# Reading the high part of the experts' inner values from the product bank, with a second gelu

## The chip, the cores and the metric

The kernel runs on one core of a Trainium2 chip. The metric is the device time of one execution in microseconds, lower is better. One execution is also recorded by the hardware profiler; all times of engines below come from that record, counted from the start of its span.

## The reference

Two sequences of 1024 rows of 256 numbers go through a first attention layer, a layer norm, a second attention with 16 heads of 128, and a mixture of four experts. The change touches only the experts:

```python
hmid = gelu(einsum('td,edi->tei', x, we1) + be1, approximate=False)   # E = 4, inner 256
eout = einsum('tei,eid->ted', hmid, we2) + be2
out  = einsum('te,ted->td', comb, eout)       # comb: weights of the two best experts, 0 elsewhere
return h + out
```

## The kernel before

The kernel is written engine by engine: each engine has a list of steps in a fixed order, and semaphores (`Event`) tie them together. Every product is made of values split in two: a high part in fp32r and a low part, the fp32 value less the high part. `product` issues three matmuls for one product (high by high, high by low, low by high).

After the attention comes the experts' stage. For each batch `b` (2) and each unit `u` (8: four experts for each of the two chunks of 512 rows) there are

- `expert_in(b, u)` on TensorE (PE): two halves, each of 6 matmuls into one bank of `ps_m`, which holds 128 inner values of the 512 rows. The halves are numbered n = 2u and 2u + 1.
- `middle(b, u)` on ScalarE (ACT), four instructions in this order: `gelu_mid(2u)`, `gelu_mid(2u+1)` (L1088: gelu of the bank plus bias, written in fp32 to the SBUF tile `gelu`, which lies in `work`), then `high_mid(2u)`, `high_mid(2u+1)` (L1100: the high part, from `gelu` to `mid_part(0, ...)`, which lies in `wqk_hi` for even u and in `qk_hi` for odd u).
- `low_mid(b, n)` on GpSimd (POOL, L2107): `gelu` less the high part.
- `expert_out(b, u)` on PE: two halves of 12 matmuls into `ps_s`. It needs the low parts of its unit.
- `mix_bias` (L1656) and `mix` (L1666) on VectorE (DVE): add the bias and the weighted result to `acc`.

`ps_m` has two banks, and all of PE's products that go there take them in turn: expert halves, the gate's logits (`gate_logits`, L620), the transposes of a layer norm (`ln_transpose`, L477), the last head's output (`outputs`). `take_bank` numbers the uses. The use of number k waits until use k - 2 has been read, by the event that the table `freed` names for its kind; for `"mid"` that is the end of `gelu_mid` of that half.

Two more waits matter. `gelu_mid(n)` waits for `low_mid(n-2)`, since `gelu` holds two halves. `high_mid` of a unit waits for `expert_out` of the unit but one before it (`out_mm`), whose high parts lie in the same place.

The order on PE around the stage, written out by hand in `ends()`: in(0,0), a transpose, in(0,1), `outputs(LAST, 1)`, out(0,0), two output projections, `ln_transpose(5, 0)`, out(0,1), in(0,2), `gate_logits(1, 0)`, in(0,3), in(0,4), out(0,2), `ln_transpose(5, 1)`, out(0,3), `gate_logits(1, 1)`, in(0,5), out(0,4), in(0,6), out(0,5), in(0,7), out(0,6), in(1,0), in(1,1), out(0,7), in(1,2), out(1,0), out(1,1), in(1,3), out(1,2), in(1,4), in(1,5), out(1,3), out(1,4), in(1,6), out(1,5), in(1,7), out(1,6), out(1,7).

Of the kernel before, what the change touches and what calls it, by code (L numbers as in the profile page):

```python
# [11 lines left out]
ACT = mybir.ActivationFunctionType  # L12
# [8 lines left out]
EXPERTS, INNER = 4, 256  # L21
# [80 lines left out]
def build(nc, A):  # L102

    with ExitStack() as ctx:
# [6 lines left out]
        def event(name, order, step=1):  # L111
            return Event(sem(name), list(order), step)
# [18 lines left out]
        be1 = vec[:, 12:20].rearrange("p (e i) -> p e i", i=2)  # L131
# [26 lines left out]
        gelu = work[:, 0:2, :]  # L158
# [72 lines left out]
        fold_lo = event("fold_lo", folds)  # L231
# [64 lines left out]
        o_lo = event("o_lo", outs2)  # L296
        rinv_done = event("rinv_done", [(u, c) for u in range(UNITS) for c in range(NC)])
        wo_mm = event("wo_mm", outs4)
        acc_done = event("acc_done", first4 + outs4)
# [5 lines left out]
        gate_got = event("gate_got", chunks)  # L305
# [5 lines left out]
        gelu_done = event("gelu_done", mids)  # L311
        mid_hi_done = event("mid_hi_done", mids)
# [60 lines left out]
        def mid_part(n, u, i):  # L373
            if u % 2 == 0:
                whole = (wqk_hi, wqk_lo)[n][:, :, :, :, :].rearrange("p h j k n -> p (h j k n)")
                return whole[:, i * CH:(i + 1) * CH]
            return (qk_hi, qk_lo)[n][:, 1, 0, i * CH:(i + 1) * CH]
# [3 lines left out]
        def m_bank(*use):  # L381
            return ps_m[:, shared[use] % 2, :]
# [13 lines left out]

        @block.tensor
        def _(pe):
            freed = {"fold": fold_lo, "gate": gate_got, "pv": o_lo, "pvs": acc_done, "wo": acc_done, "mid": gelu_done}

            def take_bank(*use):

# [522 lines left out]
        def _(act):  # L925
# [165 lines left out]
            def high_mid(b, n):  # L1091
                u = n // 2
                act.wait_ge(gelu_done.sem, gelu_done.at(b, n))
                if 8 * b + u >= 2:
                    act.wait_ge(out_mm.sem, 16 * b + 2 * (u - 1))
                elif u == 1:
                    act.wait_ge(s_mm.sem, s_mm.at(LAST, NT - 1))
                else:
                    act.wait_ge(qk_mm.sem, qk_mm.at(LAST, 3))
                act.activation(mid_part(0, u, n % 2), gelu[:, n % 2, :],  # L1100
                               ACT.Copy).then_inc(mid_hi_done.sem, mid_hi_done.up(b, n))

            def middle(b, u):
                gelu_mid(b, 2 * u)
                gelu_mid(b, 2 * u + 1)
                high_mid(b, 2 * u)
                high_mid(b, 2 * u + 1)
# [1366 lines left out]
```

## Time and profile before

| | |
|---|---|
| time, median of 3 runs | 1152.41 us (1150.47 to 1155.04) |
| time of the profiled execution | 1155.01 us |
| its span | 1152.9 us |
| PE busy over the span | 1121.9 us (97%), 7154 matmuls |
| DVE, ACT, POOL busy | 866.1 us (75%), 736.6 us (64%), 637.8 us (55%) |
| chain that ended last | PE 91%, DVE 5% |
| experts' stage | from about 1034 us to the end |

The profiled execution took 2.1 us more than its span, and 2.6 us more than the median. Busy time of PE is that of pipelined matmuls, each counted until its modelled end, so it says where PE stands still rather than how well it is used.

### The profile page before, as it was taken

The page shows a single profiled execution, that of the slowest core. Times are in us where ns is not written, and L with a number is a line of the kernel's source. Part 1 is how long each engine was busy: PE and PEld are TensorE (multiplying, and loading weights), DVE is VectorE, ACT ScalarE, POOL GpSimd, SP SyncE. Part 2 cuts the span into 40 slices and gives each one's busy share as a digit, 9 for nine tenths or more (in the row PEclk, how much of TensorE's full clock was granted, in tenths as well). Part 3 has the DMA queues.
Part 4 walks back from the last instruction along what each step waited for, and adds up shares of the span by engine and source line. Part 5 has one row for each costly group of instructions (what it writes and reads, how often), then busy time and mean ns, then how long its engine had stood idle before and what let it go on. Part 6 is the DMA issues. An engine that isn't in the chain of part 4 may idle for free.

```text
span 1152.9 us, 20493 instructions
## 1 busy us (share of the span) xinstructions
PE 1121.9 (97%) x7154; PEld 1021.8 (89%) x7154; DVE 866.1 (75%) x2016; ACT 736.6 (64%) x1565; POOL 637.8 (55%) x511
## 2 busy tenths in 40 slices
PE   8999999999999999999999999999999999889996
PEld 7998889999999999899999999999999998777995
DVE  6766877777777777777777777777777767867698
ACT  3746766666666666666666666666666665574753
POOL 2225756555655555656555555555555556845663
PEclk9999999999999999999999999999999999899998
DMA  5002222121212121212121212121212111221001
GB/s 170 1 1 78 63 73 55 41 60 38 51 38 60 38 51 38 60 38 51 38 60 37 51 37 61 38 51 38 60 37 51 42 38 46 65 92 37 1 20 55
DMA packets 46301, 56.55 MB, mean 49 GB/s; under 512 B 5940, under 2 KB 29176, under 8 KB 46200
## 3 DMA queue, kind: packets, MB, share of 16 engines
q1 hardware_dynamic: 45368, 54.19, 18.9%
q8 instruction: 58, 0.95, 0.3%
q10 hardware_dynamic: 832, 1.05, 0.3%
q14 instruction: 43, 0.35, 0.1%
HBM read 17.47 MB, written 4.19 MB: 19 GB/s over the span
## 4 chain that ended last, share of the span: by engine, by line
PE 91%; DVE 5%; issue 1%; POOL 1%; ACT 1%; DMA 0%; SPq 0%; POOLq 0%; DVEq 0%; ACTq 0%
PE ps_m L424 56%; PE ps_s L424 22%; PE ps_t L562 11%; PE ps_m L477 1%; PE ps_t L430 1%; DVE acc L1595 1%; DVE rows L1487 0%; DVE pT_lo L1562 0%; DVE stats L1434 0%; PE ps_m L620 0%; DVE acc L1666 0%; DVE ps_s L1555 0%; DVE work L1516 0%; DMA wst<-in_L_ffn_we 0%; DVE acc L1477 0%
## 5 line engine op out<-in xcount | busy, mean ns | idle before, releaser
L2069 POOL TENSOR_TENSOR work<-work,rope 128x512 f32<-128x512 f32 x128 | 166.8, 1303 | 229.2 <-DMA work<-work 229.2
L1562 DVE TENSOR_TENSOR pT_lo<-ps_t,pT_hi 128x512 fp32r<-128x512 f32 (+3 forms) x408 | 210.5, 550 | 40.9 <-ACT pT_hi L1065 38.4
L1065 ACT ACTIVATE pT_hi<-ps_t 128x512 fp32r<-128x512 f32 (+3 forms) x408 | 183.0, 489 | 74.9 <-PE ps_t L562 74.5
L1555 DVE CUSTOM_DVE_ANT_0 ps_s<-ps_s,causal 128x128 f32<-128x128 f32 (+7 forms) x272 | 203.2, 765 | 5.9 <-PE ps_s L424 3.3
L2080 POOL TENSOR_TENSOR qk_lo<-work,qk_hi 128x512 fp32r<-128x512 f32 x128 | 163.0, 1293 | 24.9 <-ACT qk_hi L1022 24.9
L2073 POOL TENSOR_TENSOR work<-work 128x512 f32<-128x512 f32 x128 | 167.4, 1308 | 10.1
L1595 DVE SCALAR_TENSOR_TENSOR acc<-ps_m,rinv,acc 128x256 f32<-128x256 f32 x272 | 118.5, 477 | 61.2 <-PE ps_m L424 61.1
L1016 ACT ACTIVATE work<-ps_m,bqk 128x512 f32<-128x512 f32 x128 | 88.7, 693 | 114.5 <-PE ps_m L424 114.3
L424 PE MATMUL ps_s<-qk_hi 128*128 128x384 f32 (+5 forms) x384 | 140.8, 367 | 2.0 <-POOL qk_lo L2080 1.2
L1058 ACT ACTIVATE prob_b<-ps_s,nmax 128x640 f32<-128x640 f32 (+3 forms) x136 | 130.3, 958 | 19.5 <-DVE nmax L1555 16.1
L424 PE MATMUL ps_m<-pT_hi,v_hi 128*128 128x512 f32 (+2 forms) x384 | 135.2, 352 | 3.4 <-DVE pT_lo L1562 2.5
L424 PE MATMUL ps_m<-pT_lo,v_hi 128*128 128x512 f32 (+2 forms) x384 | 134.1, 349 | 0.0
L424 PE MATMUL ps_m<-pT_hi,v_lo 128*128 128x512 f32 (+2 forms) x384 | 133.9, 349 | 0.0
L424 PE MATMUL ps_s<-qk_lo,qk_hi 128*128 128x384 f32 (+5 forms) x384 | 131.8, 343 | 0.0
L424 PE MATMUL ps_s<-qk_hi,qk_lo 128*128 128x384 f32 (+5 forms) x384 | 131.1, 341 | 0.0
L1516 DVE SCALAR_TENSOR_TENSOR work<-ps_m,bqk,rope 128x512 f32<-128x512 f32 x128 | 95.4, 745 | 47.0 <-ACT work L1016 46.8
L562 PE MATMUL ps_t<-ident,prob_b 128*128 128x128 f32 x884 | 120.3, 275 | 1.6 <-DVE pT_lo L1562 1.5
L562 PEld LDWEIGHTS ps_t<-ident,prob_b 128*128 128x128 f32 x884 | 101.9, 141 | 11.4 <-issue 2.9
L1022 ACT ACTIVATE qk_hi<-work 128x512 fp32r<-128x512 f32 x128 | 79.2, 641 | 40.6 <-POOL work L2073 40.4
L424 PE MATMUL ps_m<-hT_hi,wqk_hi 128*128 128x512 f32 x256 | 103.6, 405 | 0.0
L424 PE MATMUL ps_m<-hT_hi,wqk_lo 128*128 128x512 f32 x256 | 100.8, 394 | 0.0
L424 PE MATMUL ps_m<-hT_lo,wqk_hi 128*128 128x512 f32 x256 | 100.6, 393 | 0.0
(197 smaller groups left out, 2855.2 us busy)
## 6 DMA issues: line engine op xcount, KB each, us to landing
work<-work SPq DMA_DIRECT2D x256, 128.0 KB, 2.3
acc<-in_L_attn_x SPq DMA_DIRECT2D x8, 256.0 KB, 4.4
wst<-in_L_ffn_wq SPq DMA_DIRECT2D x16, 128.0 KB, 2.5
wst<-in_L_ffn_wk SPq DMA_DIRECT2D x16, 128.0 KB, 2.4
wo_st<-in_L_ffn_wo SPq DMA_DIRECT2D x16, 128.0 KB, 2.1
wst<-in_L_ffn_wv SPq DMA_DIRECT2D x8, 256.0 KB, 3.0
x_rows<-acc SPq DMA_DIRECT2D x4, 512.0 KB, 3.5
wst<-in_L_ffn_we SPq DMA_DIRECT2D x8, 256.0 KB, 2.9
```

The source lines that it names most:

```text
L424: ins = pe.matmul(out, lhs[x], rhs[y], start=first and k == 0, stop=last and k == 2)
L562: last = pe.transpose(t_bank(u, i, j)[:, k * P:(k + 1) * P], probs(i)[:, part], ident[:, :])
L1016: act.activation(qb[:, x % 2, :], m_bank("q", u, x), ACT.Identity, bias=bqk[:, j, head_:head_ + 1]).then_inc(qb_done.sem, qb_done.up(u, x))
L1058: act.activation(probs(i), all_scores[:, score_range(i)], ACT.Exp, bias=nmax[:, u % 2, i:i + 1], scale=-1.0, accum_out=rsum[:, u % 2, i:i ...
L1065: act.activation(pT_hi[:, slots, cols], t_bank(u, i, j)[:, 0:size * P].rearrange("p (j q) -> p j q", q=P), ACT.Copy).then_inc(t_hi.sem, t_ ...
L1516: dve.scalar_tensor_tensor(qc[:, ring3(u, x), :], m_bank("q", u, x), bqk[:, j, head_:head_ + 1], cos_t[:, c * CH:(c + 1) * CH], ALU.add, A ...
L1555: dve.tensor_tensor_reduce(s, s, causal[:, T - (i + 1) * P:T], -1.0, ABOVE_ALL, ALU.add, ALU.min, accum_out=nmax[:, u % 2, i:i + 1]).then_ ...
L1562: dve.tensor_tensor(pT_lo[:, slots, cols], t_bank(u, i, j)[:, 0:size * P].rearrange("p (j q) -> p j q", q=P), pT_hi[:, slots, cols].bitcas ...
L1595: last = dve.scalar_tensor_tensor(acc[:, b, tile, :], src[:, t * D:(t + 1) * D], rinv[:, u % 2, tile:tile + 1], acc[:, b, tile, :], ALU.mu ...
L2069: pool.tensor_tensor(qs[:, x % 2, :], qs[:, x % 2, :], sin_t[:, c * CH:(c + 1) * CH], ALU.mult).then_inc(sin_done.sem, sin_done.up(u, x))
L2073: pool.tensor_tensor(qc[:, ring3(u, x), :], qc[:, ring3(u, x), :], qs[:, x % 2, :], ALU.add).then_inc(rope_done.sem, rope_done.up(u, x))
L2080: pool.tensor_tensor(qk_lo[:, u % 2, j, cols], qc[:, ring3(u, x), :], qk_hi[:, u % 2, j, cols].bitcast(F32), ALU.subtract).then_inc(qk_lo_ ...
```

## The change

The high part is no longer converted from the fp32 result in SBUF. It is made by a second gelu of the same bank with the same bias, whose output is fp32r. The first gelu stays, because POOL needs its fp32 result for the low part. The bank is therefore read twice, and it counts as free only when the second reading is done.

```diff
-            freed = {"fold": fold_lo, ..., "mid": gelu_done}
+            freed = {"fold": fold_lo, ..., "mid": mid_hi_done}
...
-                act.activation(mid_part(0, u, n % 2), gelu[:, n % 2, :],
-                               ACT.Copy).then_inc(mid_hi_done.sem, mid_hi_done.up(b, n))
+                act.activation(mid_part(0, u, n % 2), m_bank("mid", b, n), ACT.Gelu,
+                               bias=be1[:, u % EXPERTS, n % 2:n % 2 + 1]).then_inc(mid_hi_done.sem, mid_hi_done.up(b, n))
```

No engine gets another order. What differs is what 32 uses of a bank on PE wait for, and what 32 instructions on ACT read. On PE, at the end of in(0,2), with the gate's logits and in(0,3) behind it (a row is an instruction or several alike; the names in brackets are the semaphores it waits for):

```order
 L424 MATMUL ps_m<-hT_lo,qk_hi 128x512
 L424 MATMUL ps_m<-hT_hi,qk_lo 128x512
-L620 MATMUL ps_m<-w_gate,hf 128x4 [waits ln_f,gelu_done]
+L620 MATMUL ps_m<-w_gate,hf 128x4 [waits ln_f,mid_hi_done]
 L620 MATMUL ps_m<-w_gate,hf 128x4 x7
-L424 MATMUL ps_m<-hT_hi,qk_hi 128x512 [waits gelu_done,we_lo]
+L424 MATMUL ps_m<-hT_hi,qk_hi 128x512 [waits mid_hi_done,we_lo]
 L424 MATMUL ps_m<-hT_lo,qk_hi 128x512
 L424 MATMUL ps_m<-hT_hi,qk_lo 128x512
```

The gate's first matmul takes the bank of in(0,2)'s first half, and in(0,3) that of the second half; both now wait for the high part of it. On ACT, units (0,2) and (0,3):

```order
 L1088 ACTIVATE work<-ps_m,vec 128x512 [waits mid_lo_done,mid_mm] x2
-L1100 ACTIVATE wqk_hi<-work 128x512 [waits out_mm,gelu_done] x2
-L1088 ACTIVATE work<-ps_m,vec 128x512 [waits mid_lo_done,mid_mm] x2
-L1100 ACTIVATE qk_hi<-work 128x512 [waits out_mm,gelu_done] x2
+L1100 ACTIVATE wqk_hi<-ps_m,vec 128x512 [waits out_mm,gelu_done] x2
+L1088 ACTIVATE work<-ps_m,vec 128x512 [waits mid_lo_done,mid_mm] x2
+L1100 ACTIVATE qk_hi<-ps_m,vec 128x512 [waits out_mm,gelu_done] x2
```

The two instructions of L1100 stand where they stood, behind both gelus of their unit and behind the same waits; only their source and function differ.

## Rows read from the trace of the kernel before

**Rows 1.** Busy time by stretch, 1034 us to the end; PEclk is the granted clock.

```profile
1034.00:1082.00 48.00, 45.40 (x285) 40.39 (x284) 28.29 (x71) 28.32 (x47) 31.14 (x22) 0.96 0.08 23
1082.00:1126.00 44.00, 44.00 (x283) 40.16 (x282) 42.70 (x104) 25.94 (x42) 28.26 (x21) 1.00 0.04 13
1126.00:1153.00 27.00, 15.49 (x104) 13.76 (x102) 23.56 (x64) 8.77 (x16) 9.52 (x9) 0.86 0.17 59
```

**Rows 2.** Waits, 1034 us to the end: total us, times, longest.

```profile
ACT work L1088 <- PE ps_m L424: 22.9, 18, 3.1
...
PE ps_s L424 <- POOL wqk_lo L2107: 0.5, 1, 0.5
```

**Rows 3.** Groups of instructions, 1034 us to the end: busy us, mean ns.

```profile
L1656 DVE SCALAR_TENSOR_TENSOR acc<-work,comb,acc 128x256 f32<-128x256 f32 x64 | 37.6, 646 | 0.3
L1666 DVE SCALAR_TENSOR_TENSOR acc<-ps_s,comb,acc 128x256 f32<-128x256 f32 x64 | 26.8, 475 | 4.6 <-PE ps_s L424 4.3
...
L1088 ACT ACTIVATE work<-ps_m,vec 128x512 f32<-128x512 f32 x32 | 22.0, 689 | 33.1 <-PE ps_m L424 22.9 <-POOL wqk_lo L2107 8.1 <-POOL qk_lo L2107 2.0
...
L1100 ACT ACTIVATE wqk_hi<-work 128x512 fp32r<-128x512 f32 x16 | 9.2, 622 | 1.9 <-PE ps_s L424 1.9
```

**Rows 4.** Order of time on ACT: high parts of units (0,2), (0,3), (1,3).

```profile
1061.23 1.14 ACT L1100 ACTIVATE wqk_hi<-work 128x512 fp32r<-128x512 f32 x2
...
1065.79 1.14 ACT L1100 ACTIVATE qk_hi<-work 128x512 fp32r<-128x512 f32 x2
...
1113.38 1.14 ACT L1100 ACTIVATE qk_hi<-work 128x512 fp32r<-128x512 f32 x2
```

**Rows 5.** Order of time on PE: `gate_logits(1, 0)`, first matmuls of in(0,4) and in(1,4).

```profile
1060.44 0.95 PE L620 MATMUL ps_m<-w_gate,hf 128*128 128x4 f32 x8
...
1065.01 0.39 PE L424 MATMUL ps_m<-hT_hi,qk_hi 128*128 128x512 f32 x1
...
1115.47 0.40 PE L424 MATMUL ps_m<-hT_hi,qk_hi 128*128 128x512 f32 x1
```

**Rows 6.** Order of time on ACT: high parts of units (0,1), (0,4) and (1,1).

```profile
1043.47 1.14 ACT L1100 ACTIVATE qk_hi<-work 128x512 fp32r<-128x512 f32 x2
...
1070.86 1.15 ACT L1100 ACTIVATE wqk_hi<-work 128x512 fp32r<-128x512 f32 x2 [0.76 <-PE ps_s L424]
...
1101.61 1.16 ACT L1100 ACTIVATE qk_hi<-work 128x512 fp32r<-128x512 f32 x2 [0.29 <-PE ps_s L424]
```

**Rows 7.** Order of time on PE: `outputs(LAST, 1)`, `ln_transpose(5, 1)`, out(0,3), in(1,2).

```profile
1042.33 0.47 PE L424 MATMUL ps_m<-pT_hi,v_hi 128*128 128x512 f32 x1 [2.09 <-DVE pT_lo L1562]
...
1070.60 1.03 PE L477 MATMUL ps_m<-ident,rows 128*128 128x128 f32 x8
1071.39 0.36 PE L424 MATMUL ps_s<-v_hi,qk_hi 128*128 128x256 f32 x1
...
1101.35 0.40 PE L424 MATMUL ps_m<-hT_hi,qk_hi 128*128 128x512 f32 x1
```

**Rows 8.** Order of time on DVE: start of `gating_2(1)`, and `mix(1, 7, 0)`.

```profile
1082.39 0.19 DVE L1614 TENSOR_REDUCE g<-prob 128x8 f32<-128x32 f32 x1 [1.61 <-ACT prob L1112]
...
1144.30 0.88 DVE L1666 SCALAR_TENSOR_TENSOR acc<-ps_s,comb,acc 128x256 f32<-128x256 f32 x2
```

**Rows 9.** Order of time on PE: first matmul of out(1,7).

```profile
1139.84 0.38 PE L424 MATMUL ps_s<-v_hi,qk_hi 128*128 128x256 f32 x1 [0.95 <-POOL qk_lo L2107]
```

**Rows 10.** Busy time by short stretch, columns as in the first group.

```profile
136.00:139.00 3.00, 1.19 (x6) 0.67 (x5) 3.00 (x4) 2.72 (x7) 2.34 (x3) 1.00 0.39 87
139.00:142.00 3.00, 3.00 (x20) 2.73 (x20) 2.61 (x7) 1.41 (x3) 2.19 (x2) 1.00 0.00 0
...
995.00:996.50 1.50, 0.46 (x4) 0.25 (x3) 1.50 (x5) 1.50 (x4) 1.50 (x2) 1.00 0.81 242
...
999.00:1002.00 3.00, 3.00 (x16) 3.00 (x15) 1.97 (x6) 2.22 (x4) 2.92 (x3) 0.50 0.14 48
...
1043.20:1046.60 3.40, 3.40 (x10) 2.62 (x9) 2.37 (x6) 1.42 (x3) 3.00 (x3) 0.50 0.93 292
```

More of the change, by code:

```diff
@@ L398, in _ @@
         def _(pe):
-            freed = {"fold": fold_lo, "gate": gate_got, "pv": o_lo, "pvs": acc_done, "wo": acc_done, "mid": gelu_done}
+            freed = {"fold": fold_lo, "gate": gate_got, "pv": o_lo, "pvs": acc_done, "wo": acc_done, "mid": mid_hi_done}
             def take_bank(*use):
```

## The prediction

> **What bounds the kernel now.** I looked first at the busy time by stretch, because the change touches only the experts' stage, the last 119 us. PE is busy 45.4 of 48 us from 1034 to 1082, and all of the 44 us from 1082 to 1126; DVE is busy 28.3 us in the first of these stretches and 42.7 in the second [rows 1]. So there are two regimes. Up to 1082 PE alone sets the pace. Behind that PE is still full, but DVE is 97% busy too, and it may be DVE that sets the end.
>
> The waits come next. ACT stood idle 22.9 us in this stage for the products of PE, 18 times [rows 2]. PE itself waited there for nothing on ACT: the first gelu empties a bank in time for its next use. ACT has room, then, and work added to ACT costs nothing by itself. What counts is when a bank comes free.
>
> Last, the order of time on ACT beside that on PE, use by use: for each use of a `ps_m` bank behind an expert half, does the high part end before or after PE got there? Before the change this did not matter. After it, each use where it ends later is a stall.
>
> **The second gelu's duration.** The trace has this operation already: a gelu from the bank with a bias takes 689 ns, the copy it replaces 622 ns [rows 3]. The output type is the only difference. I take 0.69 us, 0.07 us more than before, 32 times: 2.1 us on an engine that idles. From both sides: not less than the 0.62 of the copy, and not more than 0.78, if fp32r output cost as much again as the difference of the two. Per stall the two ends are 0.07 and 0.09 us off.
>
> The Trainium skill, "VectorE: DVE Perf Modes", section on the TRN2 errata, says that ScalarE needs 224 cycles plus one for each element when it reads SBUF, and only 172 when it reads PSUM; by that rule the new instruction would be 43 ns shorter than the copy instead of 67 ns longer, and the seven stalls below together some 0.8 us cheaper. The trace disagrees about this kernel's two forms: the one that reads the bank is the slower by 67 ns. The rows decide here.
>
> **When a bank comes free.** Before, the first bank of a unit was free at the end of its own gelu. Now ACT first does the second gelu of the unit and then the high part. When PE goes straight on to the next expert half, it arrives before that. With L the start of the pair of high parts, the first bank is free at L + 0.69, the second 0.6 later. To each stall I add 0.16 us: 0.06 from the release to the first matmul, and 0.1 until the matmuls stream at full pace again, both estimates from how PE restarts behind its present waits. At `outputs(LAST, 1)` PE stood waiting already, so only the 0.06 counts there.
>
> - `gate_logits(1, 0)` behind in(0,2): high parts start at 1061.23 [rows 4], so the bank is free at 1061.92; PE was there at 1060.44 [rows 5]. 1.48, with restart 1.64.
> - in(0,4) straight behind in(0,3): 1065.79 + 0.69 = 1066.48 [rows 4] against 1065.01 [rows 5]. 1.47, with restart 1.63.
> - in(1,1) behind in(1,0) and in(1,5) behind in(1,4) are the same pattern, an `expert_in` straight behind another with ACT on time: 1.63 each.
> - `ln_transpose(5, 1)` stands behind out(0,2), and the high parts of (0,4) wait for that very out(0,2) [rows 6]. Banks free at 1070.86 + 0.69 = 1071.55 and at 1072.15. The eight transposes go from 1070.60 to 1071.39 [rows 7]; the second four can't start before 1072.15 and take 0.4, so out(0,3) starts at 1072.55 instead of 1071.39. 1.16, with restart 1.3.
> - in(1,2) behind out(0,7), in the same way: 1101.61 + 0.69 = 1102.30 [rows 6] against 1101.35 [rows 7]. 0.95, with restart 1.1.
> - `outputs(LAST, 1)` takes the bank of (0,1)'s first half. Its gelus had waited for POOL, so its high parts start only at 1043.47 [rows 6]; free at 1044.16, and PE started at 1042.33, behind 2.09 us of waiting for a low part on DVE [rows 7]. 1.83, with 0.06 1.9. in(0,1) also stalls, some 0.7 us, but that lies inside this wait.
>
> All other uses are covered by an `expert_out` of some 2.9 us between two `expert_in`; in(1,4) is one: its bank is free at 1113.38 + 0.69 = 1114.07 [rows 4], and PE comes at 1115.47 [rows 5], 1.4 us later. If ACT were later than now by that much, they would stall too.
>
> The sum on PE is 1.64 + 1.63 + 1.63 + 1.63 + 1.3 + 1.1 + 1.9 = 10.8 us.
>
> **What is given back at the end.** 6.5 us of this (the first, the second, the fifth and the last item) come before 1082.39, where DVE begins an unbroken run to the end, released by ACT and so, through the logits, by PE [rows 8]. They move the end by their full size. The other 4.4 us meet a DVE that was behind PE: `mix(1, 7, 0)` began at 1144.30 [rows 8], while its product, 1.4 us of matmuls from 1139.84 [rows 9] with some 0.3 us until DVE sees it, was there at 1141.5. That is a reserve of 2.8 us. A DVE that catches up also releases POOL sooner, which made PE wait 0.5 us [rows 2]. But DVE doesn't catch up freely: `mix_bias` takes 646 ns a piece on average against 475 of the like instruction of `mix` [rows 3], held up where POOL is at work, and the last low parts on POOL move with PE. I take the 0.5 and 1 of the 2.8. From both sides: nothing back, or all of the 4.4, where DVE alone sets the end.
>
> That makes 10.8 - 1.5 = 9.3 us.
>
> **The clock.** A PE that stands still can lose its clock. After a stretch with 0.46 us of matmuls in 1.5, the clock was granted at 0.50 in 999 to 1002; after the wait at 1042.33 it was 0.50 for 3.4 us, in which 1.7 us of work are lost. But after 1.19 us of matmuls in 3 at 136 to 139 it stayed at 1.00 [rows 10]. So a stop of about 1.5 us may or may not cost 1.7 us. The likeliest place is the gate: a stop of 1.6 us and right behind it the logits' matmuls, 4 columns wide. I count one such drop, 1.7 us. The bounds are none and three. The low clock behind `outputs(LAST, 1)` is paid for before the change as well.
>
> **Sum.** 9.3 + 1.7 = 11.0 us. The profiled execution would go from a span of 1152.9 to about 1164, and from 1155.0 to 1166. That execution lies 2.6 us over the median, so against the median of 1152.4 the forecast is 1163.4 us.
>
> **Rivals.**
> - *DVE sets the end, and no clock is lost.* Only the 6.5 us ahead of DVE's unbroken run count. 1159 us. For it: 42.7 us busy of 44. Against it: PE was only some 2 to 5 us ahead of DVE, the later stalls are 4.4, and the last low parts hang on PE.
> - *The stops cost the clock again and again.* Two or three drops in place of one, and nothing given back: 10.8 + 3.4 to 5.1, so 1166.6 to 1168.3 us. For it: seven stops of more than 1 us, one of them before and one inside sparse transposes. Against it: the expert matmuls around the other stops are dense.
> - *No difference.* ACT idles, PE's queue absorbs the later release, 1152.4 us. It decides if the high part ended before PE came, or within 0.1 us of it. At seven places the rows say 0.95 to 1.83 us later.
> - *Faster.* One mechanism: PE's pauses end the meetings of DVE and POOL in SBUF. The 64 pieces of `mix_bias` take 0.17 us more than those of `mix`, 11 us in all [rows 3]. If all of it vanished and DVE alone set the end, it would be 6.5 - 11 = 4.5 us faster, 1148 us. It decides above 6.5 us saved, and no work leaves POOL or DVE, so half of it would already be much.
>
> **Chances.** Forecast as told, with one or no drop of the clock and 0 to 3 us given back: 0.58. DVE sets the end: 0.16. Repeated drops: 0.16. No difference: 0.08. Faster: 0.02. The range reaches from the first rival to the second, 1158 to 1168.5 us. A measurement of this kernel can tell about 0.5%, 5.8 us, from no change, so slower begins at 1158.2, and a part of the DVE rival falls short of it: slower 0.88, same 0.10, faster 0.02.
>
> **What the profile after would show.** Right: waits of PE for L1100 on ACT, seven of 1 to 2 us and an eighth of 0.7 at in(0,1), about 10 us in sum and none behind an `expert_out` that stands between two `expert_in` (but for in(1,2)). L1100 at 0.69 us with `ps_m` as its source. DVE's first step behind the gate's exponentials at about 1089 to 1091 instead of 1082.39. The clock at 0.5 for some 3 us near 1064. DVE a little nearer to PE at the end. Wrong: L1100 far from 0.69; other places for the stalls, above all if ACT drifts and the covered uses stall too; or DVE with the same times relative to 1082.39 up to the end, which would be the first rival. What I trust least is the clock, then what DVE gives back.

## The result and the profile after

The changed kernel takes 1165.64 us, median of 4 runs (1163.07 to 1166.80), against 1151.82 us for the kernel before in the same comparison. The ratio is 1.0113, with a 95% interval from 1.0092 to 1.0135: 13.8 us slower, between 10.6 and 15.5. The profiled execution has a span of 1162.5 us. The median lies 2.2 us above the forecast and inside its range.

First the waits of PE in the profile after, from 1020 us to the end (total us, times, longest):

```profile
PE ps_m L424 <- ACT qk_hi L1100: 5.5, 3, 3.2
PE ps_m L424 <- ACT wqk_hi L1100: 3.3, 3, 1.4
PE ps_m L620 <- ACT wqk_hi L1100: 1.4, 1, 1.4
...
PE ps_s L424 <- POOL qk_lo L2107: 1.1, 1, 1.1
...
PE ps_m L477 <- ACT wqk_hi L1100: 0.8, 1, 0.8
```

Before, PE did not wait for L1100 or L1088 once in this stretch; its only wait on ACT was one of 0.8 us in the attention (for L1058), which is there after the change too. Now there are eight on L1100, 11.0 us. The order of time on PE shows where (seven of them had been worked out; the rows of before are in [rows 5, 7]):

```profile
1029.56 0.48 PE L424 MATMUL ps_m<-hT_hi,qk_hi 128*128 128x512 f32 x1
...
1034.06 0.47 PE L424 MATMUL ps_m<-hT_hi,qk_hi 128*128 128x512 f32 x1 [0.57 <-ACT wqk_hi L1100]
...
1040.26 0.80 PE L424 MATMUL ps_m<-pT_hi,v_hi 128*128 128x512 f32 x1 [3.20 <-ACT qk_hi L1100]
...
1059.90 0.39 PE L620 MATMUL ps_m<-w_gate,hf 128*128 128x4 f32 x2 [1.36 <-ACT wqk_hi L1100]
...
1069.35 0.47 PE L424 MATMUL ps_m<-hT_hi,qk_hi 128*128 128x512 f32 x1 [1.45 <-ACT qk_hi L1100]
...
1076.04 1.24 PE L477 MATMUL ps_m<-ident,rows 128*128 128x128 f32 x8 [0.84 <-ACT wqk_hi L1100]
...
1102.92 0.50 PE L424 MATMUL ps_m<-hT_hi,qk_hi 128*128 128x512 f32 x1 [1.36 <-ACT wqk_hi L1100]
...
1109.66 0.50 PE L424 MATMUL ps_m<-hT_hi,qk_hi 128*128 128x512 f32 x1 [0.84 <-ACT qk_hi L1100]
...
1128.15 0.50 PE L424 MATMUL ps_m<-hT_hi,qk_hi 128*128 128x512 f32 x1 [1.36 <-ACT wqk_hi L1100]
...
1149.45 0.39 PE L424 MATMUL ps_s<-v_hi,qk_hi 128*128 128x256 f32 x1 [1.10 <-POOL qk_lo L2107]
```

In order: the start of in(0,0), in(0,1), `outputs(LAST, 1)`, `gate_logits(1, 0)`, in(0,4), `ln_transpose(5, 1)`, in(1,1), in(1,2), in(1,5), and out(1,7). The stage began 4.0 us earlier in this execution than in that of before (in(0,0) at 1033.57 there), mostly because the attention ahead of it, which the change doesn't touch, had met less of the low clock (from 995 us on 3.4 us of it, against 10.2 before, which is 3.4 of the 4.0 us). So I count all places from in(0,0): how much later than before each is reached.

| reached | us later than before | added there |
|---|---|---|
| `outputs(LAST, 1)` | 1.9 | 1.9 |
| `gate_logits(1, 0)` | 3.5 | 1.5 |
| in(0,4) | 8.4 | 1.5 by the wait, 3.4 by the clock |
| out(0,3) | 9.7 | 1.3 with the restart |
| in(1,1) | 11.2 | 1.5 |
| in(1,2) | 12.3 | 1.2 |
| in(1,5) | 13.9 | 1.6 |
| out(1,7) | 13.6 | -0.3 |
| end of the span | 13.6 | 0 |

The second gelu itself, from the instructions of L1100 in the profile after:

```profile
L1100 ACT ACTIVATE wqk_hi<-ps_m,vec x16: 680/685/693, 1033.2 to 1140.9; 128x512 fp32r<-128x512 f32 x16
```

685 ns. Busy time by stretch shows the clock behind the gate, and that DVE now has pauses between 1082 and 1126 us, 40.10 us busy of 44 where it was 42.70 before (the columns are those of [rows 1]):

```profile
1060.80:1067.60 6.80, 6.80 (x22) 5.57 (x21) 1.82 (x6) 0.69 (x1) 1.61 (x2) 0.50 0.00 0
...
1082.00:1126.00 44.00, 41.80 (x262) 37.43 (x261) 40.10 (x106) 26.03 (x39) 23.22 (x18) 1.00 0.02 7
```

For 6.8 us PE had the clock at 0.50, the lower of its two levels, 1.2 GHz. It worked through, and so lost 3.4 us. The low began 0.9 us after the gate's logits had started, behind the stop of 1.36 us. In the profiles of all four kernels in which PE stands still there (this one, and below those with the release alone, with batch 0 alone and with the change and a lighter DVE) a low of 6.8 us follows. Of the ten profiles in which PE does not wait for a bank at the gate, eight have no low there and two have one of 3.4 us.

Last, DVE from the start of its run to the end, to be read beside [rows 8]:

```profile
1088.16 0.18 DVE L1614 TENSOR_REDUCE g<-prob 128x8 f32<-128x32 f32 x1 [1.74 <-ACT prob L1112]
...
1114.22 0.88 DVE L1666 SCALAR_TENSOR_TENSOR acc<-ps_s,comb,acc 128x256 f32<-128x256 f32 x2 [0.73 <-PE ps_s L424]
1115.66 0.87 DVE L1666 SCALAR_TENSOR_TENSOR acc<-ps_s,comb,acc 128x256 f32<-128x256 f32 x2 [0.56 <-PE ps_s L424]
...
1134.98 3.76 DVE L1656 SCALAR_TENSOR_TENSOR acc<-work,comb,acc 128x256 f32<-128x256 f32 x4
...
1145.10 1.65 DVE L1666 SCALAR_TENSOR_TENSOR acc<-ps_s,comb,acc 128x256 f32<-128x256 f32 x4
1146.78 3.69 DVE L1656 SCALAR_TENSOR_TENSOR acc<-work,comb,acc 128x256 f32<-128x256 f32 x4
...
1153.91 0.88 DVE L1666 SCALAR_TENSOR_TENSOR acc<-ps_s,comb,acc 128x256 f32<-128x256 f32 x2
```

`mix(1, 7, 0)` begins 4.46 us after out(1,7), exactly as before (1144.30 less 1139.84). At the end nothing of that lag had been used up, though DVE's run had started only 9.8 us later and PE reached out(1,7) 13.6 us later. In between it was: at 1114.22 and 1115.66 DVE had caught up with PE and waited for its products, 1.3 us in two waits; before the change it waited for none in this stretch. Then it fell behind again at pieces of `mix_bias` beside low parts on POOL. Those of (1,4), at 1134.98, take 3.76 us, where the same four took 1.66 before:

```profile
1127.63 1.66 DVE L1656 SCALAR_TENSOR_TENSOR acc<-work,comb,acc 128x256 f32<-128x256 f32 x4
```

Four more, at 1146.78 beside the last low parts on POOL, take 3.69 us, where they took 3.54 before. In all, the 64 pieces of the stage take longer than the 37.6 us of [rows 3], by the groups of instructions of the changed kernel:

```profile
L1656 DVE SCALAR_TENSOR_TENSOR acc<-work,comb,acc 128x256 f32<-128x256 f32 x64 | 40.3, 689 | 0.3
```

### The profile page after: what moved, and what is told of

The parts are those of the page before. It is cut to its first block, busy times and chain, and to the rows that moved or that the text cites. A ratio compares the mean times of both kernels' runs of the same rounds, so it can differ in the third digit from the quotient of the medians.

```text
span 1162.5 us, 20493 instructions
## 1 busy us (share of the span) xinstructions
PE 1123.3 (97%) x7154; PEld 1020.1 (88%) x7154; DVE 867.0 (75%) x2016; ACT 739.2 (64%) x1565; POOL 637.3 (55%) x511
## 4 chain that ended last, share of the span: by engine, by line
PE 91%; DVE 5%; issue 1%; ACT 1%; POOL 1%; DMA 0%; POOLq 0%; DVEq 0%; SPq 0%; ACTq 0%
PE ps_m L424 56%; PE ps_s L424 23%; PE ps_t L562 11%; DVE rows L1487 1%; PE ps_m L477 1%; PE ps_m L620 1%; DVE acc L1595 1%; DVE pT_lo L1562 0%; DMA acc<-in_L_attn_x 0%; DVE work L1516 0%; DVE ps_s L1555 0%; DVE stats L1434 0%; DVE acc L1477 0%; ACT qk_hi L1100 0%; ACT wqk_hi L1100 0%
## 5 line engine op out<-in xcount | busy, mean ns | idle before, releaser
L1058 ACT ACTIVATE prob_b<-ps_s,nmax 128x640 f32<-128x640 f32 (+3 forms) x136 | 130.4, 959 | 19.7 <-DVE nmax L1555 16.3
L424 PE MATMUL ps_s<-qk_hi,qk_lo 128*128 128x384 f32 (+5 forms) x384 | 130.9, 341 | 0.0
L562 PE MATMUL ps_t<-ident,prob_b 128*128 128x128 f32 x884 | 119.4, 273 | 2.1 <-DVE pT_lo L1562 1.9
```

The source lines that it names most:

```text
L424: ins = pe.matmul(out, lhs[x], rhs[y], start=first and k == 0, stop=last and k == 2)
L562: last = pe.transpose(t_bank(u, i, j)[:, k * P:(k + 1) * P], probs(i)[:, part], ident[:, :])
L1058: act.activation(probs(i), all_scores[:, score_range(i)], ACT.Exp, bias=nmax[:, u % 2, i:i + 1], scale=-1.0, accum_out=rsum[:, u % 2, i:i ...
```

## The experiments

All were timed against the kernel before. "Stage" is the profiled execution's span from the start of in(0,0), "low" the time in it at the lower clock until PE's work ends, and the last column is the stage less half of the low, that is without what the clock costs. This takes the noise of the attention out of the comparison. Half of the low is an upper bound of its cost where PE stood still in a part of it, as in the two kernels with the other order on ACT and the two changed ones with filled stops (by 0.3 to 0.4 us in the latter). The ratio is not the quotient of the two medians: the two columns agree within 1 us for most kernels, and differ by 1.0 to 1.9 us for the two with a lighter DVE and the changed one with two stops filled.

| kernel | ratio to before, 95% | median us over before | stage us | low us | stage without the clock's cost |
|---|---|---|---|---|---|
| before | | | 119.3 | 3.4 | 117.6 |
| changed | 1.0113 [1.0092, 1.0135] | 13.8 | 132.9 | 10.2 | 127.8 |
| release alone | 1.0110 [1.0088, 1.0132] | 13.4 | 132.3 | 10.2 | 127.2 |
| duration alone | 0.9995 [0.9979, 1.0012] | -0.3 | 117.7 | 0 | 117.7 |
| batch 1 alone | 1.0040 [1.0025, 1.0056] | 5.0 | 123.2 | 3.4 | 121.5 |
| batch 0 alone | 1.0082 [1.0062, 1.0102] | 9.7 | 127.6 | 6.8 | 124.1 |
| changed, other order on ACT | 1.0076 [1.0052, 1.0099] | 8.9 | 128.7 | 10.2 | 123.6 |
| before, other order on ACT | 1.0041 [1.0026, 1.0057] | 4.4 | 123.0 | 3.4 | 121.3 |
| changed, one stop filled | 1.0099 [1.0076, 1.0122] | 11.3 | 130.9 | 6.8 | 127.5 |
| changed, four banks | 1.0017 [1.0003, 1.0031] | 2.5 | 121.1 | 3.4 | 119.4 |
| before, lighter DVE | 0.9949 [0.9929, 0.9969] | -6.9 | 114.3 | 0 | 114.3 |
| changed, lighter DVE | 1.0092 [1.0072, 1.0112] | 8.7 | 130.1 | 10.2 | 125.0 |
| changed, two stops filled | 1.0091 [1.0071, 1.0111] | 9.0 | 129.4 | 3.4 | 127.7 |
| before, its stop filled | 0.9989 [0.9976, 1.0003] | -1.7 | 117.4 | 0 | 117.4 |

**The release of the bank alone.** The copy from SBUF stays; only the table changes.

```diff
-            freed = {..., "mid": gelu_done}
+            freed = {..., "mid": mid_hi_done}
```

> The high part is copied from the first gelu's result as before; only the release of the bank waits for it. Theory (the late release is the cause): nearly all of the change's 13.8 us stay, 12 to 14 us over before, since each of the seven stalls is only 0.07 us shorter. Rival (the longer instruction on ScalarE, or its second reading of the bank, is the cause): within 2 us of before.

Measured 13.4 us, with the eight waits at the same places, each 0.04 to 0.07 shorter (the copy takes 0.62), and the same low clock of 6.8 us behind the gate. This one word makes all of the loss but 0.6 us by the profiles (132.3 against 132.9); the rival falls.

**The duration alone.** The bank is free as before, the instruction is longer.

```diff
-                act.activation(mid_part(0, u, n % 2), gelu[:, n % 2, :],
-                               ACT.Copy)...
+                act.activation(mid_part(0, u, n % 2), gelu[:, n % 2, :], ACT.Identity,
+                               bias=zero[:, 0:1])...
```

> The bank is released as before; the high part is made from the first gelu's result by an Identity with a bias of zeros, an instruction as long as the second gelu or longer (0.69 to 0.78 us). Theory (late release): within 1 us of before. Rival (duration on ScalarE): most of the 13.8 us.

Measured -0.3 us, an interval that holds 0. In the profile of this kernel L1100 is even longer than the second gelu:

```profile
L1100 ACT ACTIVATE wqk_hi<-work,zero x16: 711/714/724, 1033.2 to 1125.3; 128x512 fp32r<-128x512 f32 x16
```

3 us of added work on ACT, 32 times 0.09, cost nothing.

**Each batch by itself.**

```diff
+NEW = (1,)      # (0,) for batch 0 alone
...
+                        if kind == "mid" and key[0] in NEW:
+                            empty = mid_hi_done
...
+                if b in NEW:
+                    act.activation(mid_part(0, u, n % 2), m_bank("mid", b, n), ACT.Gelu, ...)
+                else:
+                    act.activation(mid_part(0, u, n % 2), gelu[:, n % 2, :], ACT.Copy)...
```

> The change only for the second batch, so only the stalls at in(1,1), in(1,2) and in(1,5), 4.3 us on TensorE, are left. Theory as read after the result (VectorE gives back next to nothing): 3.5 to 4.3 us over before. Theory as forecast: 2.8 us. Rival (VectorE sets the end from 1082 us on): 0 to 1 us.

> The change only for the first batch: stalls at outputs(LAST,1), gate_logits(1,0), in(0,4), ln_transpose(5,1), 6.3 us, and the low clock behind the gate, 3.4 us if it lasts as long as in the profile of the changed kernel. Theory: 9.5 us over before with a low clock of 6.8 us behind the gate, 8 us with one of 3.4, 6.3 us with none. It and the run with batch 1 alone should add up to the whole change, 13.8 us.

Batch 1 costs 5.0 us in the median, between 2.9 and 6.4 by its interval, and 3.9 us in the profile, where both executions had the same low clock. That rules out that DVE sets the end from 1082 us on (0 to 1 us), and in the profile 4.3 us of stalls come out as 3.9. The 2.8 us of the forecast lie just outside the interval, and 1.1 us under what the profile shows. Batch 0 costs 9.7 us, as expected with its low clock of 6.8 us. In the medians the two add up to 14.7 us against 13.8. Without the clock's share they are 3.9 and 6.5 us, in sum 10.4, and the whole change is 10.2 us.

**Another order on ACT**, in the changed kernel and in the kernel before:

```diff
                 gelu_mid(b, 2 * u)
-                gelu_mid(b, 2 * u + 1)
                 high_mid(b, 2 * u)
+                gelu_mid(b, 2 * u + 1)
                 high_mid(b, 2 * u + 1)
```

> The change with ScalarE's four instructions of a unit in another order: gelu and high part of the first half, then gelu and high part of the second. The first bank is free 0.6 us earlier than the end of the first high part now, 1.3 us. Theory (the stalls are the release against TensorE's arrival): the four places with an expert_in or the gate straight behind shrink from 1.5 to 0.2 us each, outputs(LAST,1) loses its 1.9, in(1,2) keeps 1.1, ln_transpose(5,1) grows to 1.9; 4 us over before, no low clock behind the gate. Rival (the second reading of the bank is what costs, in whatever order): 10 us or more over before.

> The kernel before with the same new order on ScalarE, and nothing else. Theory: TensorE hardly waits for ScalarE there, so within 1 us of before, perhaps 0.5 us faster by earlier low parts at the end. Rival (the order itself is worth something): 1.5 us or more either way.

Both missed, the first by 4.9 us and the second by 3.4 beyond its bound: the order has a price of its own, 4.4 us in the kernel before (3.7 in the profile, without the clock), which is the rival of the second run. The difference between the two kernels in this order is 4.5 us in the medians and 2.4 without the clock, against 13.8 and 10.2 in the old order. So the stalls did shrink as the theory wants. Of PE's waits on ACT in the changed kernel with this order, two are left at `ln_transpose(5, 1)`, 1.12 and 0.64 us, and one at in(1,2), 0.84. The theory had overlooked the order's price; and it was wrong on the clock, since a low of 3.4 us lies behind the gate although PE did not wait ahead of it. Where the price goes is seen, in the profile of the kernel before with the new order, in PE's waits. PE waits 3.04 us on POOL, 1.84 on DVE's `mix` and 1.20 on a gelu at `ln_transpose(5, 1)`, where it waited 1.5 us on POOL and on the other two not at all. Behind the first stand DVE and POOL. Groups of instructions, 1030 us to the end:

```profile
L1656 DVE SCALAR_TENSOR_TENSOR acc<-work,comb,acc 128x256 f32<-128x256 f32 x64 | 45.5, 771 | 0.3
```

Order of time on POOL, the last but two low parts and the power behind a norm's variance:

```profile
1130.06 1.42 POOL L2107 TENSOR_TENSOR wqk_lo<-work,wqk_hi 128x512 fp32r<-128x512 f32 x1 [3.29 <-ACT wqk_hi L1100]
1135.92 1.17 POOL L2036 TENSOR_TENSOR rstd<-var,minus_half 128x4 f32<-128x4 f32 x1 [4.44 <-DVE var L1440]
1137.07 1.48 POOL L2107 TENSOR_TENSOR wqk_lo<-work,wqk_hi 128x512 fp32r<-128x512 f32 x1
```

Order of time on PE in the same kernel, the first matmul of out(1,6):

```profile
1138.61 0.58 PE L424 MATMUL ps_s<-v_hi,wqk_hi 128*128 128x256 f32 x1 [3.04 <-POOL wqk_lo L2107]
```

`mix_bias` takes 771 ns a piece in place of 646 [rows 3], 8 us in all. The variance that a norm needs comes later from DVE, POOL stands still 4.44 us for it with the next low part queued behind, and PE waits 3.04 us for that low part, where it was 0.5 before [rows 2]. A guess is that the low parts reach POOL one by one, so that DVE meets POOL's work more often. Neither this nor how much of the 3.7 us it makes was tested by itself.

**Four banks.** Every second unit from (0,2) on uses the two banks of `ps_t`, which nothing else needs by then; the high part is the second gelu, in the old order.

```diff
+            if use[0] == "mid" and use[1] * 8 + use[2] // 2 >= 2 and use[2] // 2 % 2 == 0:
+                return ps_t[:, use[2] % 2, :]
             return ps_m[:, shared[use] % 2, :]
...
-                    out = take_bank("mid", b, 2 * u + i)
+                    m = 8 * b + u
+                    if m >= 2 and m % 2 == 0:
+                        if m >= 4:
+                            pe.wait_ge(mid_hi_done.sem, 16 * b + 2 * (u - 2) + i + 1)
+                        out = ps_t[:, i, :]
+                    else:
+                        out = take_bank("mid", b, 2 * u + i)
```

> The changed kernel with four banks: the halves of every second unit from (0,2) on go to the two banks of ps_t, which nothing else uses by then. The high part is still a second gelu of the bank, the order is the same. Theory (the release meets the next use of the bank): all stalls but the one at outputs(LAST,1) and the one hidden at in(0,1) are gone, 1.9 us over before. Rival (reading the bank twice costs something besides): more than 4 us over before.

2.5 us in the median, between 0.3 and 3.6 by its interval, and 1.8 in the profile. PE's waits on ACT from in(0,0) on are then these two, and no other (L1108 is the high part in this kernel's lines):

```profile
PE ps_m L426 <- ACT qk_hi L1108: 3.2, 1, 3.2
...
PE ps_m L426 <- ACT wqk_hi L1108: 0.6, 1, 0.6
```

So reading a bank twice costs nothing that shows here beyond the stall that is left, forecast at 1.9 us. It costs where the next use of the bank stands close behind.

**The clock.** In the changed kernel, the stop ahead of the gate is filled with transposes whose output nobody reads; then the one ahead of `outputs(LAST, 1)` too; and in the kernel before the latter alone. `keep_busy(out, n)` issues n transposes of the identity into `out`.

```diff
+                keep_busy(ps_t[:, 0, :], 12)
                 gate_logits(1, 0)
...
+                keep_busy(ps_s[:, 3, :], 24)      # 16 in the kernel before
                 outputs(LAST, 1)
```

> The changed kernel with 12 transposes into an unused bank, 1.3 us, in place of the stop ahead of gate_logits(1,0). The stop itself is filled, not shortened. Theory (the low clock behind the gate costs 3.4 us and comes from the stop and the logits together): no low clock between 1055 and 1075 us, 10.2 us over before in place of 13.8. Rival (the low clock comes from elsewhere, or the slow matmuls were hidden by a later wait): 13.5 us or more over before.

> The changed kernel with two fillings on TensorE: 24 transposes into an unused bank in the stop ahead of outputs(LAST,1), and 12 ahead of gate_logits(1,0). Theory (the clock falls after the stops): no low clock between 1030 and 1100 us, so the stage lasts 8.5 to 9 us longer than in the profile of before, 9 us over before in the median. Rival (the fall at the first stop has another cause, or moves elsewhere): 11 us or more.

> The kernel before with 16 transposes, 1.8 us, in its stop of 2.1 us ahead of outputs(LAST,1). Theory: the low clock of 3.4 us behind that stop is gone, 1.6 us faster than before. Rival (it would not have been on the path, or comes anyway): within 0.5 us.

Busy time by stretch of the kernel with one stop filled:

```profile
1042.30:1049.10 6.80, 6.14 (x15) 4.80 (x16) 2.03 (x5) 1.19 (x3) 4.02 (x4) 0.50 0.40 136
1060.00:1075.00 15.00, 13.51 (x81) 11.52 (x80) 6.46 (x23) 8.29 (x14) 10.16 (x9) 1.00 0.00 1
```

And of the kernel with two stops filled:

```profile
1040.00:1046.00 6.00, 5.38 (x31) 4.53 (x29) 2.77 (x6) 1.84 (x3) 4.78 (x4) 1.00 0.56 174
...
1062.80:1066.20 3.40, 2.70 (x7) 1.59 (x5) 0.78 (x2) 1.34 (x3) 0.00 (x0) 0.51 0.00 0
```

With the gate's stop filled the low clock there is gone, but the low behind the first stop is 6.8 us long instead of 3.4; the stage is 2.0 us shorter, not 3.4. In the median it is 2.5 us, but its interval, from 8.8 to 14.1 us over before, holds both the theory and the rival. With both filled, the clock holds behind the first stop, and 3.4 us behind the gate are low again, now without a stop ahead of the logits. So my expectation of no low clock at all was wrong, though the 9.0 us in the median are what it gave: in this execution a low lies behind logits with no stop ahead of them, in the one before it doesn't. What holds in both is the sum. The stage without the clock's cost is 127.8, 127.5 and 127.7 us in the three, and what differs is the low time, 10.2, 6.8 and 3.4 us, at half its length. In the kernel before, the filling took away the low clock behind the stop, and the stage is 1.9 us shorter. In the medians that is -1.7 us with an interval from -2.8 to 0.3: the best version here, but not one that the timing tells from the kernel before.

**A lighter DVE.** In both kernels three of the four pieces of every `mix_bias` of batch 1 are left out.

```diff
-                for t in range(TC):
+                for t in range(1 if b else TC):
```

> The kernel before, without three of every four bias additions of the second batch (mix_bias only for the first tile of a unit: 24 instructions of VectorE are left out, 15.5 us at 646 ns; their part of the result is missing). Theory (VectorE's lag sets the last 3 us): 2 to 4 us faster than before. Rival (VectorE sets the end from 1082 us on by its whole length): 8 us or more faster. Third (TensorE alone sets the end): within 1 us.

> The changed kernel with the same additions left out. If the stalls of the second batch are partly hidden behind VectorE in the full kernel, the change costs more without VectorE's load: theory (VectorE hides 0.3 us at most): the change costs 13 to 15 us here too, so 10 to 12 us over before in all. Rival (VectorE hid 1.5 us or more, as forecast): the cost rises to 15 us or more against the run of before with the same additions left out.

24 pieces less, and the kernel before is 6.9 us faster in the median (3.6 to 8.2 by the interval). That is more than the theory's 2 to 4, and the interval reaches the rival's 8. The profiles differ by 5.0 us; 1.7 of that is the low clock that this execution didn't have, and 3.3 us are left without it. The fastest runs of the two kernels, 1145.63 and 1148.87 us, lie 3.2 us apart too. The changed kernel is 2.9 us faster without the clock's cost. So the theory holds by the profiles and not by the median: DVE's lag sets the last 3 us or so. The end in the changed and lighter kernel, order of time on DVE:

```profile
1150.99 0.88 DVE L1666 SCALAR_TENSOR_TENSOR acc<-ps_s,comb,acc 128x256 f32<-128x256 f32 x2 [1.38 <-PE ps_s L424]
```

`mix(1, 7, 0)` follows out(1,7) (at 1149.19) by 1.80 us here, 4.46 in the full kernel. The reserve of 2.7 us was really there. The cost of the change between the light kernels is 15.6 us in the medians and 15.7 in the stages. By these numbers the rival came true, with its 15 us or more. But 5.1 us of them are clock, since the lighter kernel before had no low clock in the stage: 10.6 us are left without it, against 10.2 between the full ones. So by the profiles DVE hid 0.4 us of the stalls, and not 1.5.

## Why the prediction was right

The place and the size of the stalls were worked out use by use, and they make 10.5 of the 13.6 us in the profile. The two smaller terms were both off, in the same direction, and the range held them because it had left room for more of the low clock. Of the signs named for the profile after, the eight waits, the 0.69 us of L1100 and the covered uses came out. DVE's run began 9.8 us later, not 7 to 9, by the longer low clock, and DVE was not nearer to PE at the end.

**The stalls.** Forecast 10.8 us at seven places, each from the end of the high part against PE's arrival. Measured 1.9, 1.5, 1.5, 1.3, 1.5, 1.2 and 1.6: 10.5 us, at these seven places, with the eighth hidden at in(0,1) and none at the covered uses. The reading of ACT's rows beside PE's was enough for this. The experiment with the release alone shows that the release is the cause, that with the duration alone that the duration isn't, and that with four banks that hardly anything else is behind it.

**The duration.** Taken 0.69 us, measured 0.685.

**Which rule holds.** The rule of the Trainium skill ("VectorE: DVE Perf Modes", section on the TRN2 errata) that ScalarE is quicker from PSUM was set against two forms that differ in more than the source. The experiment with the duration alone gives the third: Copy from SBUF 621 ns, Identity with a bias from SBUF 714 ns, gelu with a bias from the bank 685 ns. If the function itself makes no difference, which no run here separates, the bias costs 93 ns, and with a bias on both sides the bank is quicker by 29 ns. The table's figures would make it 43, an estimate. The Trainium skill, "ScalarE: Activation LUTs", section "What ACT_TABLE_LOAD costs", gives some 93 ns for each operand that is a pointer; the 93 ns here agree. So the direction of the rule is right, the rows of before were right for the sum, and my sentence that the trace disagrees was too strong: it had compared a form with a bias with one without.

**What is given back at the end.** Here the step failed: I took 1.5 us, of a possible 4.4, and it was 0.3. The step was "I take the 0.5 and 1 of the 2.8". The 0.5 came: PE no longer waits for POOL ahead of out(1,6), while its wait ahead of out(1,7) grew from 0.95 to 1.10. The 1 didn't, and not because DVE never caught up. Its run started 3.8 us nearer to PE's end than before. 1.3 us of this went into the two waits for PE at 1114 and 1115, and the rest, about, into pieces of `mix_bias` that had become longer: 40.3 us for the 64 in place of 37.6, those of (1,4) alone 2.1 us longer, beside POOL's low parts. The last meeting, at 1146.78, took 3.69 us as it took 3.54 before, beside low parts that follow PE's last `expert_in`. So the lag at the end is made anew by late meetings of DVE and POOL. That is a reading of the rows and not shown by a run of its own, since none moved POOL's work alone. The light kernels show that the lag is real, 2.7 us in both, and that the change costs but 0.4 us more without it.

**The clock.** The likeliest place was right, the gate, but the size was half: the low lasted 6.8 us and cost 3.4, where I had taken 1.7 from the one row of 3.4 us. The trace of before could have warned me: from 1005.7 to 1012.5 us, in the attention's last part, it has the clock at 0.50 too, in a low of 6.8 us. The 1.7 us too little here and the 1.2 us too much given back point the same way, 2.9 us together; the 0.3 us too much at the stalls goes the other way. 11.0 + 1.7 + 1.2 - 0.3 = 13.6 us, what the profile shows. Whether the low lasts 3.4 or 6.8 us could not have been told from the rows of before; that one such low was counted, and at this place, was a choice and not a derivation.

**The rivals.** DVE as the one that sets the end from 1082 falls with batch 1 alone (5.0 us, where it had 0 to 1). Repeated drops came true in part: the low was twice as long, but at one place. No difference and faster fall with the result; of the 11 us that the meetings of DVE and POOL cost, nothing was saved, and `mix_bias` grew from 646 to 689 ns a piece.

## What to carry to other kernels

Before a buffer is held longer, list every later use of it and read the two times side by side: when its last reader would now end, and when the writer arrives in the trace. An engine with idle time can take more instructions for nothing, but not one more instruction between a product and the release of its bank. And an engine that lags behind the critical one may be no reserve, if its lag is made anew by meetings with a third engine whose work moves with the critical one: look at what the lag consists of before you subtract it. Here 0.3 us of 2.8 were given back.

## What was not expected of the hardware

- The clock is worth several us of noise and of effect here. The profiled executions that can be compared fit stage = fixed work + half of the time at the lower clock: three variants of the changed kernel agree within 0.3 us without it, with 10.2, 6.8 and 3.4 us low, and so do the kernel before, that with the duration alone and that with its stop filled (117.6, 117.7 and 117.4), with 3.4, 0 and 0. Filling one stop removed the low clock behind it, and the one behind an earlier stop was twice as long in that execution. Where a low clock falls, and for how long, I could only bound, not forecast; why is open.
- The order of two instructions on an idle engine cost 4.4 us (1.0041, 1.0026 to 1.0057), and the pieces of `mix_bias` grew from 646 to 771 ns with it. That these make the cost is likely but was not tested. The Trainium skill ("SBUF — State Buffer", section "Who interferes with whom") says that a DVE instruction with two SBUF inputs contends with a GpSimd instruction that reads SBUF; the trace agrees as far as it goes, since the pieces of `mix`, with one input from PSUM, stay at 477 ns in the same kernel.
- An ACT instruction with a bias from SBUF takes 93 ns more than a Copy at 128x512 (714 against 621), three times what the source in PSUM saves with a bias on both sides (29).
